# A two-layer macaron network on one core: attention's layer-norm statistics move from POOL to VectorE, and the SSM's output products, norms and ring steps are re-timed

## The reference

```
x = x + 0.5 * moe_ffn(layernorm(x))     # 8 experts, top 2, exact gelu
x = x + ssm(layernorm(x))               # Mamba-like, 32 heads, state 64, R = 2, chunks of 128
x = x + 0.5 * moe_ffn(layernorm(x))
x = x + 0.5 * lora_moe(layernorm(x))    # base + top 2 of 8 low-rank experts (2 null ones)
x = x + attention(layernorm(x))         # 16 heads of 8, q and k normalized, causal
x = x + 0.5 * lora_moe(layernorm(x))

layernorm(x) = (x - mean) / sqrt(var + 1e-5)
# the SSM's end, per token:
y = y_intra + y_inter;  y = rms(y * silu(z));  out = y @ W_out
```

## Time and profile before

| | |
|---|---|
| median of 3 runs | 1444.87 us (1443.93 to 1449.31) |
| profiled execution | 1445.81 us |
| its span | 1444.1 us |
| mean granted PE clock | 0.856 |
| busy: PE, DVE, ACT, POOL | 81%, 72%, 56%, 53% |

### The profile page before, as it was taken

How to read it: one execution, slowest core, us unless ns; L and a number is a source line. 1 busy time by engine, 2 the same in 40 slices (tenths; PEclk the granted TensorE clock), 3 DMA queues, 4 the chain that set the end, 5 groups by cost and what they waited for, 6 DMA issues and landing times. The chain is left out here.

```text
span 1444.1 us, 32988 instructions
## 1 busy us (share of the span) xinstructions
PE 1166.5 (81%) x11380; PEld 739.8 (51%) x11380; DVE 1036.0 (72%) x2301; ACT 804.3 (56%) x1477; POOL 760.8 (53%) x1115
## 2 busy tenths in 40 slices
PE   7679963698988989889757996358998998898894
PEld 6369952455545545555636995343443444343332
DVE  6959973888888897899786997574756766673433
ACT  3768854445235325411346885026777677787881
POOL 2366633763674675355346664557547565544421
PEclk6779986698889989999658998557999999999997
DMA  8025340000000000000412333000000010000000
GB/s 280 18 88 178 90 60 22 22 9 2 23 9 2 19 13 1 2 2 2 138 61 68 90 90 54 20 15 16 9 15 12 5 31 10 7 8 9 1 16 8
DMA packets 55714, 55.09 MB, mean 38 GB/s; under 512 B 9882, under 2 KB 44484, under 8 KB 55556
## 3 DMA queue, kind: packets, MB, share of 16 engines
q1 hardware_dynamic: 46468, 34.37, 7.6%
q0 software_dynamic: 9088, 18.63, 5.8%
HBM read 32.26 MB, written 20.71 MB: 37 GB/s over the span
## 5 line engine op out<-in xcount | busy, mean ns | idle before, releaser
L2146 ACT ACTIVATE l_probs<-l_ps 128x1024 f32<-128x1024 f32 (+1 forms) x320 | 287.8, 947 | 100.4 <-PE l_ps L2032 99.8
L784 POOL DMA_INDIRECT ffn_yg<-y_rows,ffn_index x156 | 156.3, 1002 | 82.6 <-PE ffn_ps_t L799 39.4
L2051 PE MATMUL l_ps<-l_probs,l_vs 128*32 128x512 f32 (+3 forms) x1536 | 165.6, 520 | 30.2 <-POOL l_probs L2228 22.7
L2228 POOL TENSOR_SCALAR_AFFINE_SELECT l_probs<-l_probs 128x256 f32<-128x256 f32 x256 | 110.1, 449 | 140.5 <-ACT l_probs L2146 139.5
L867 ACT ACTIVATE ffn_hT<-ffn_ps_h,experts_b1T,experts_scales 128x256 f32<-128x256 f32 x312 | 151.1, 563 | 30.7 <-PE ffn_ps_h L814 29.4
L266 POOL DMA_INDIRECT combine_og<-o_rows,combine_place x128 | 139.9, 1093 | 51.4 <-issue 27.6
L1310 PE MATMUL ssm_ps<-ssm_X,ssm_near 32*32 32x256 f32 x2048 | 138.3, 422 | 1.9 <-DVE ssm_Y L1753 1.9
L2032 PE MATMUL l_ps<-l_qkT 32*128 32x512 f16 (+3 forms) x768 | 109.3, 339 | 16.0 <-ACT l_probs L2146 13.9
L1552 POOL TENSOR_TENSOR ssm_u_out<-ssm_ysum,ssm_zx 128x256 f32<-128x256 f32 x32 | 69.0, 2156 | 99.8 <-DVE ssm_ysum L1764 99.7
L892 DVE SCALAR_TENSOR_TENSOR ffn_h<-ffn_hT,experts_scales,ffn_h 128x512 f16<-128x512 f32 x156 | 117.2, 752 | 5.5
L830 PE MATMUL ffn_ps_o<-experts_w,ffn_h 128*128 x624 | 113.1, 220 | 2.2 <-DVE ffn_h L892 2.0
(11 more groups left out here) (354 smaller groups left out, 2865.6 us busy)
## 6 DMA issues: line engine op xcount, KB each, us to landing
o_rows<-ffn_out_sb SPq DMA_DIRECT2D x78, 128.0 KB, 2.1
y_rows<-ffn_y SPq DMA_DIRECT2D x8, 512.0 KB, 5.1
kept_w<-experts_w SPq DMA_DIRECT2D x16, 256.0 KB
experts_w<-kept_w SPq DMA_DIRECT2D x16, 256.0 KB, 5.9
ffn_yg<-y_rows,ffn_index POOLq DMA_INDIRECT x156
x_res<-in_L_attn_x SPq DMA_DIRECT2D x4, 512.0 KB, 6.1
prep_raw<-in_L_ffn_W SPq DMA_DIRECT2D x1, 2048.0 KB, 10.4
prep_raw<-in_L_ffn_W SPq DMA_DIRECT2D x8, 256.0 KB, 5.6
```

The lines of the kernel that those rows point to most:

```text
L784: g_.indirect_dma_start(yg[:, i % RING, j].rearrange("p n d -> p (n d)"), None, w.y_rows.ap(), bass.IndirectOffsetOnAxis(ap=index[:, n:n + ...
L2051: ins = t_.matmul(ps_o[VP * h:VP * h + VP, q0 % H:q0 % H + width], vs[:, s % 2, kb, h, :], probs[:, n % PSLOTS, i, at:at + width], start=( ...
L2146: s_.activation(probs[:, w % PSLOTS, i:i + n, 0:width], ps_s[w % 2][:, i:i + n, 0:width], ACT.Exp, scale=SCALE / (UNIT * UNIT)).then_inc(S ...
L2228: g_.affine_select(p, p, [[0, n], [1, P]], ALU.is_ge, 0.0, base=0, channel_multiplier=-1).then_inc(S["m_done"], 1)
```

## The change

Two stages change, each for itself.

**SSM.** From the third group on, the group's whole norm stream starts two steps earlier, while its projections stay at the steps they had (`TURN`). `project_out` goes from step 21 to 22.6 and `finish` from 23.5 to 25. The ring is told that the "vn" use is held to step 21 instead of 18.6. `LATER[n]` puts the dots, near_levels and far_levels of a tile later where the ring moved its transposes by more than 1.5 steps; it comes out as 4.0 for tiles 6, 14 and 22 and 0 for all others.

**Attention.** The means and variances of the 24 norms are now computed by DVE (`spread`), seven operations with two waits for DVE's own results, placed directly behind the counting; POOL only does the power, at step 2.

```diff
+        TURN = [NORM + (2 if g >= 2 else 0) for g in range(GROUPS)]
-        G_AT = [C_AT[g // 2] - (46 if g % 2 else 68 if g else 55.9) for g in range(GROUPS)]
+        G_AT = [C_AT[g // 2] - (46 if g % 2 else 68 if g else 55.9) - (TURN[g] - NORM) for g in range(GROUPS)]
...
-            streams["r", n] = K[n], [(("r", n), 21, 23.5)]
+            streams["r", n] = K[n], [(("r", n), 22.6, 25)]
+        LATER = [max(0, uses.at(("t", n), -16) - (K[n] - 16) - 1.5) for n in range(TILES)]
...
                 def project(g):
-                    yield NORM + 6
+                    yield TURN[g] + 6
...
                 def dots(n):
-                    yield -14
+                    yield -14 + LATER[n]
...
                 def project_out(n):
-                    yield 21
+                    yield 22.6
...
                 def near_levels(n):
-                    yield -12
+                    yield -12 + LATER[n]
...
                 def finish(n):
-                    yield 23.5, ("r", n)
+                    yield 25, ("r", n)
...
             @block.gpsimd
                 def norm(i, g):
-                    yield 0
...
+                    yield 2
                     ts = group(g)
-                    g_.tensor_tensor(half, even, odd, ALU.subtract).then_inc(chain.sem, 1)
-                    g_.tensor_tensor(mean, even, odd, ALU.add).then_inc(chain.sem, 1)
-                    chain.n += 2
-                    chain.link(g_.tensor_tensor(var, core.stats[:, ts, 2], core.stats[:, ts, 5], ALU.add))
-                    chain.link(g_.tensor_tensor(half, half, half, ALU.mult))
-                    g_.tensor_scalar(mean, mean, 0.5, None, ALU.mult).then_inc(chain.sem, 1)
-                    g_.tensor_scalar(half, half, 0.25, None, ALU.mult).then_inc(chain.sem, 1)
-                    chain.n += 2
-                    pool.wait_ge(chain.sem, chain.n)
-                    yield 1.5
-                    chain.link(g_.tensor_scalar(var, var, 1.0 / D, LN_EPS, ALU.mult, ALU.add))
-                    chain.link(g_.tensor_tensor(var, var, half, ALU.add))
-                    g_.tensor_tensor(core.rstd[:, ts], var, core.minus_half[:, 0:GROUP], ALU.pow).then_inc(S[f"rstd{i}"], 1)
+                    pool.wait_ge(S[f"spread{i}"], g + 1)
+                    g_.tensor_tensor(core.rstd[:, ts], core.tmp2[:, ts], core.minus_half[:, 0:GROUP], ALU.pow).then_inc(S[f"rstd{i}"], 1)
...
                     ins.then_inc(S[f"counted{i}"], 1)
+                    dve.wait_ge(S[f"counted{i}"], g + 1)
+                    spread(i, g)
+                def spread(i, g):
+                    v.tensor_tensor(half, even, odd, ALU.subtract).then_inc(chain.sem, 1)
+                    v.tensor_tensor(mean, even, odd, ALU.add).then_inc(chain.sem, 1)
+                    v.tensor_tensor(var, core.stats[:, ts, 2], core.stats[:, ts, 5], ALU.add).then_inc(chain.sem, 1)
+                    chain.n += 3
+                    dve.wait_ge(chain.sem, chain.n)
+                    v.tensor_tensor(half, half, half, ALU.mult).then_inc(chain.sem, 1)
+                    v.tensor_scalar(mean, mean, 0.5, None, ALU.mult).then_inc(chain.sem, 1)
+                    v.tensor_scalar(var, var, 1.0 / D, LN_EPS, ALU.mult, ALU.add).then_inc(chain.sem, 1)
+                    chain.n += 3
+                    dve.wait_ge(chain.sem, chain.n)
+                    chain.link(v.scalar_tensor_tensor(var, half, 0.25, var, ALU.mult, ALU.add))
+                    dve.sem_inc(S[f"spread{i}"], 1)
```

More of the change, by code:

```diff
@@ L1160, in ssm @@
         for g in range(GROUPS):
-            streams["g", g] = G_AT[g], [(("g", g, "y"), NORM + 6, NORM + 8)] + [(("g", g, j), NORM + 10 + 1.5 * j, NORM + 12 + 1.5 * j) for j in range(GROUP)]
+            streams["g", g] = G_AT[g], [(("g", g, "y"), TURN[g] + 6, TURN[g] + 8)] + [(("g", g, j), TURN[g] + 10 + 1.5 * j, TURN[g] + 12 + 1.5 * j) for j in range(GROUP)]
             streams["x", g] = X_AT[g], [(("x", g, k), step, step + 2) for k, step in widths(g)]
         for b in range(BATCHES):
-            streams["c", b] = C_AT[b], [(("c", b, 0), 9, 13.5), (("c", b, 1), 10.5, 14.8), (("c", b, "ang"), 12, 16), (("c", b, "vn"), 13.2, 18.6),
+            streams["c", b] = C_AT[b], [(("c", b, 0), 9, 13.5), (("c", b, 1), 10.5, 14.8), (("c", b, "ang"), 12, 16), (("c", b, "vn"), 13.2, 21),
                                         (("c", b, 2), 14, 18), (("c", b, 3), 15.5, 19.3)]
@@ L1214, in project @@
                     for j in range(GROUP):
-                        yield NORM + 10 + 1.5 * j
+                        yield TURN[g] + 10 + 1.5 * j
                         uses.wait_read(pe, ("g", g, "y"))
@@ L1283, in dots @@
                         if r:
-                            yield -13
+                            yield -13 + LATER[n]
                             pe.wait_ge(S["s_done"], 2 * n + 1)
@@ L1379, in project @@
                     ins.then_inc(S["y_ready"], 1)
-                    yield NORM + 8, ("g", g, "y")
+                    yield TURN[g] + 8, ("g", g, "y")
                     ps = uses.wait(act, ("g", g, "y"))
@@ L1385, in project @@
                     for j in range(GROUP):
-                        yield NORM + 12 + 1.5 * j, ("g", g, j)
+                        yield TURN[g] + 12 + 1.5 * j, ("g", g, j)
                         ps = uses.wait(act, ("g", g, j))
@@ L1390, in project @@
                         uses.read(s_.copy(raw[:, h * GROUP + j, :], ps[:, 0:RAW]), ("g", g, j))
-                    yield NORM + 19
+                    yield TURN[g] + 19
                     for j in range(GROUP):
@@ L1477, in far_levels @@
                 def far_levels(n):
-                    yield -10.8
+                    yield -10.8 + LATER[n]
                     act.wait_ge(S["near_ready"], n + 1)
@@ L1588, in project @@
                         dve.sem_inc(S["spread"], 1)
-                    yield NORM + 22.5
+                    yield TURN[g] + 22.5
                     dve.wait_ge(S["squared"], g + 1)
@@ L1933, in layer1 @@
         ps_o = bank[:, 4, :]
-        names = ("dve_chain pool_chain act_chain const_ready zeroed counted0 counted1 counted2 rstd0 rstd1 rstd2 y0 y1 y2 left0 left1 "
+        names = ("dve_chain act_chain const_ready zeroed spread0 spread1 spread2 counted0 counted1 counted2 rstd0 rstd1 rstd2 y0 y1 y2 left0 left1 "
                  "exp0 exp1 zw0 zw1 base0 base1 z0 z1 x1 x2 x3 qk_taken v_taken squared ss_ready norm_ready qn_ready hi_ready split_ready "
@@ L2171, in _ @@
             def _(pool):
-                chain = Chain(pool, S["pool_chain"])
                 def norm(i, g):
-                    yield 0
[L2176 to L2179, removed]
-                    ts = group(g)
-                    even, odd = core.stats[:, ts, 1], core.stats[:, ts, 4]
-                    half, var, mean = core.tmp1[:, ts], core.tmp2[:, ts], core.mean[:, ts]
-                    g_.tensor_tensor(half, even, odd, ALU.subtract).then_inc(chain.sem, 1)
-                    g_.tensor_tensor(mean, even, odd, ALU.add).then_inc(chain.sem, 1)
-                    chain.n += 2
-                    chain.link(g_.tensor_tensor(var, core.stats[:, ts, 2], core.stats[:, ts, 5], ALU.add))
-                    chain.link(g_.tensor_tensor(half, half, half, ALU.mult))
-                    g_.tensor_scalar(mean, mean, 0.5, None, ALU.mult).then_inc(chain.sem, 1)
-                    g_.tensor_scalar(half, half, 0.25, None, ALU.mult).then_inc(chain.sem, 1)
-                    chain.n += 2
-                    pool.wait_ge(chain.sem, chain.n)
-                    yield 1.5
-                    chain.link(g_.tensor_scalar(var, var, 1.0 / D, LN_EPS, ALU.mult, ALU.add))
-                    chain.link(g_.tensor_tensor(var, var, half, ALU.add))
-                    g_.tensor_tensor(core.rstd[:, ts], var, core.minus_half[:, 0:GROUP], ALU.pow).then_inc(S[f"rstd{i}"], 1)
+                    yield 2
+                    ts = group(g)
+                    pool.wait_ge(S[f"spread{i}"], g + 1)
+                    g_.tensor_tensor(core.rstd[:, ts], core.tmp2[:, ts], core.minus_half[:, 0:GROUP], ALU.pow).then_inc(S[f"rstd{i}"], 1)
                 def heads(g):
@@ L2261, in count @@
                     ins.then_inc(S[f"counted{i}"], 1)
+                    dve.wait_ge(S[f"counted{i}"], g + 1)
+                    spread(i, g)
+                def spread(i, g):
+                    ts = group(g)
+                    even, odd = core.stats[:, ts, 1], core.stats[:, ts, 4]
+                    half, var, mean = core.tmp1[:, ts], core.tmp2[:, ts], core.mean[:, ts]
+                    v.tensor_tensor(half, even, odd, ALU.subtract).then_inc(chain.sem, 1)
[10 more added lines that the diff above has]
+                    dve.sem_inc(S[f"spread{i}"], 1)
                 def lora(i, g):
@@ L2326, in take_experts @@
                         combine.add(dve, g * GROUP + j)
+                    yield 2.8
+                    dve.wait_ge(combine.counted, (g + 1) * GROUP)
```

(1 more changed line is left out.)

## The result

| | before | after |
|---|---|---|
| median | 1446.96 us (20 runs) | 1441.18 us (20 runs) |
| profiled execution, span | 1444.1 us | 1434.5 us |
| ratio to before | | 0.995, 95% interval 0.9936 to 0.9965 |

The change saves 0.5%, some 7 us of the 22 that were forecast; the median lies just outside the range (1408 to 1441). The ratios leave out a single slow execution, one of e2's of 4335.6 us.

A forecast was written before the change was run, and what follows sets the result against it. PE (busy 81%) and DVE (72%) were taken to bound the kernel, not by the same limit everywhere. From 1445.8 us, SSM −12 and attention −10 gave 1423.8, so 1424 us; range 1408 to 1441.

The forecast's parts named there:

- The decay on DVE and its race with POOL: SSM plain tiles: DVE's decay goes before POOL's X2 when L1552 ends; period 8.80 us instead of 9.96.
- Rival C: SSM plain tiles: POOL wins at L1552's end, so a tile takes 10.73 us; total 1435 us, chance 0.17.
- The SSM's sum: All SSM terms together: −6.7 − 7.8 + 1.5 + 1.0 = −12.0 us, ends −4 and −20.
- The norms' −7.8: SSM: norms two steps earlier remove PE's two shorter waits for ssm_y, 3.95 us each, entered as −7.8 us.
- The later product: SSM, finish later: six plain tiles of the last batch gain 1.1 us each, −6.7 us.
- LATER and takes: SSM costs: late near_levels in tiles 6, 14, 22, +1.5 us; a third take in one tile per batch, +1.0 us.
- The gain on POOL: Attention: 46 us of work off POOL shortens waits for masks, with PE's clock, by 20.1 us; net −14 after costs.
- The cut, for ACT's exponentials: Attention: masks may then wait for ACT, 76% full; seven tenths of the net −14 taken, so −10 us.
- DVE is 64% full, so most fall into its pauses: Attention: 24 spreads add 26 to 31 us on DVE, mostly in pauses; total cost counted as 6 us.
- I found five such places. With 1.0 each that is +5: Attention: places where a copy stands directly behind a count, so a spread delays freeing PE's bank; +5 us.
- PE's waits for l_oTs above 10 us: Attention: sign that the prediction is wrong, PE's waits for the copy L2386 growing past 10 us.
- Rival E: Attention: spreads land on DVE's path ahead of copies, stretched to 1.8 us each, 43.2 in all; 1457 us, chance 0.08.

The follow-up runs named there:

- e2: The attention part of the change alone, SSM as before; ratio 1.0029 to the kernel before, +4 us.
- e1: The SSM part of the change alone, attention as before; ratio 0.9915 to the kernel before, −12 us.
- e8: Of the SSM part only the norms two steps earlier, product and finish at old steps, attention as before; ratio 0.9999 to the kernel before.
- e7: Of the SSM part only the later output product and finish, norms at their old steps, attention as before; ratio 0.9920 to the kernel before.
- e3: The attention part alone without the seven DVE operations of each norm (output not the reference's); ratio 0.9828 to the kernel before, −25 us.
- e5: The whole change with the spreads of norms i = 1 and 2 put 3.4 steps later; ratio 0.9831 to the kernel before, −24 us.
- e10: The whole change with only the eight spreads of norms i = 2 put 3.4 steps later; ratio 0.9861 to the kernel before, −20 us.

## Why the prediction was wrong, point by point

- **The decay on DVE and its race with POOL** was right: DVE wins at L1552's end in all six plain tiles, the decay takes 0.62 us, the period is 8.77. Rival C is out.
- **The SSM's sum** of −12 was right (e1: −12.3), but by luck: two errors cancel. The norms' −7.8 came out as nothing (e8), and the waits that were to go, 7.9 us, are still 6.2. The term was read from PE's wait for ssm_y as if that wait were all of the loss; POOL did the same work, only ahead of other work that was as urgent. The later product gave 12 (e7) against 6.7 less 2.5 for LATER and takes. Part of it is the batch's end: from tile 24's ysum to tile 31's it is 59.9 us after and 68.1 before, 8.2 less, of which 6.5 are the six plain tiles and 1.7 the last one. The rest is in the tiles with projections. There PE's wait for the product's input is nearly gone, which I had only as an end of the range; but PE waits for the input of the dots instead, which I had put at nothing. Before, and in e7:

```profile
PE ssm_ring L1358 <- ACT ssm_uT L1498: 17.2, 14, 2.9
...
PE ssm_ps L1289 <- ACT ssm_bct L1475: 2.4, 5, 0.5
```

```profile
PE ssm_ring L1361 <- ACT ssm_uT L1501: 1.4, 3, 0.5
...
PE ssm_ps L1292 <- ACT ssm_bct L1478: 15.0, 20, 2.0
```

- **The gain on POOL** was sized a little low: 20.1, with the net cut to seven tenths; it is 25 (e3). The cut, for ACT's exponentials, was the wrong way.
- **The step that failed** is "DVE is 64% full, so most fall into its pauses", with "I found five such places. With 1.0 each that is +5". The cost is 29 us (e2 against e3), not 6, by the two profiles about half of it as longer matmuls at a lower clock and half as PE idle. The window's 64% is a mean over stretches in which DVE is full and others where it idles, and a norm's statistics come, by their nature, where the residual was just finished: behind additions, in the full stretches. I looked for copies directly behind a count and not for the base additions two lines below, for which PE waits as well. And I priced PE's clock only where a long wait would go, not where short ones would come. One of the signs named for a wrong prediction did come, PE's waits for l_oTs above 10 us; but they are 10.3 in e3 without the seven too, so that sign says nothing of the spreads.
- **Rival E** was nearest to what happened, at 0.08: the spreads land on DVE's path, ahead of additions and copies. They cost 1.2 each on average and not the 1.8 it was priced at, so that attention is slower by 4 and not the whole by 11. That all 24 lie on the path is not shown. The rule of the Trainium skill (page "Perfetto Trace Analysis", section "Optimizing Scalar/DVE Operations") that spoke against moving work between DVE and GpSimd gave the right sign for this part as it stood: the trace has DVE at 8.0 more us of 100, and e2 is at 1.0029. With the same work at another place the move pays, by 12 us (e5 at 0.9831 against e1 at 0.9915). So the place decided here, and not that the work went from POOL to DVE; what share the port had in the spreads' cost no run shows.

What stays open: how e3's 25 us divide between POOL's masks and DVE's shorter wait for the power, which of the 24 places carry the 29 us besides those shown, and what the spreads of i = 0 cost, which no run moved.

## What to carry to other kernels

When work moves to an engine, list what stands directly behind each insertion and who waits for it; the busy share of a window says nothing about the place where the work falls, and statistics fall where the engine has just been busiest. An operation with slack of its own (here four steps until the power) should be given that slack in the order, not be attached to what produces its input. Where PE ran at the higher clock, two waits of 0.6 us cost it 2.9 to 4.0 us here, so short new waits can use up what a change gains by removing a long one. A term that comes out right in the sum says nothing of its parts: the SSM's −12 held only by two errors.

## What was not expected of the hardware

Two waits of PE, 0.59 and 0.64 us, stood in front of a stretch at a granted clock of 0.66, with 1.94 us for matmuls that take 1.06 at the higher level; in the same stretch of e10 the clock stayed at 1.00. The other five such pairs in three profiles went the same way (0.66 once, 0.83 four times). And the power on POOL, 1.05 us alone, took 3.50 beside DVE's 2.82 us weigh, which is longer than weigh itself: it began 0.22 us after weigh and ended 0.90 after weigh's end.
